# Quantum-style attention over 32 batches: the weighted sum over source heads as a contraction on TensorE, its operands turned through DRAM

## The reference, cut to what matters

```python
qkv = x @ W_qkv.T + b_qkv            # q, k, v: 8 heads of 16 columns each
q, k = entangle(encode(q)), entangle(encode(k))     # complex
for c in range(4):                   # circuits
    scores = g[c] * |conj(q_i) . k_j|^2             # 8 x 8 heads, for each row
    amps = sqrt(softmax(scores, over j) + 1e-12)
    weighted[i, d] = sum_j amps[i, j] * v[j, d]     # <- what the change touches
    final += sup_w[c] * clip(|weighted|, 1e-6, 1) * sign(weighted) * (sign of the sum of v over heads)
y = final @ W_out.T + b_out          # x1 = x + y
```

## Time and profile before

| | |
|---|---|
| median of 3 executions | 2482.29 us (2481.22 to 2492.06) |
| span of the profiled execution | 2447.5 us |
| PE busy | 1901.8 us, 78% |
| DVE busy | 1872.7 us, 77% |
| POOL busy | 1562.1 us, 64% |
| ACT busy | 1264.7 us, 52% |
| chain that ended last, by engine | POOL 30%, issue 25%, DVE 21%, PE 17%, ACT 6% |

### The profile page before, as it was taken

How to read it: one execution, slowest core, us unless ns; L and a number is a source line. 1 busy time by engine, 2 the same in 40 slices (tenths; PEclk the granted TensorE clock), 3 DMA queues, 4 the chain that set the end, 5 groups by cost and what they waited for, 6 DMA issues and landing times.

```text
span 2447.5 us, 42464 instructions
## 1 busy us (share of the span) xinstructions
PE 1901.8 (78%) x14044; PEld 1470.5 (60%) x14044; DVE 1872.7 (77%) x3303; ACT 1264.7 (52%) x2982; POOL 1562.1 (64%) x1233
## 2 busy tenths in 40 slices
PE   1478888888888888888888888888888877968490
PEld 0366666666666666666666666666666654746370
DVE  8989999998999999999999989999998742311010
ACT  2246666555556655555565555555555544423130
POOL 4656666666666666666666666666666215788787
PEclk9889999898999998999998989999989876989795
DMA  3000000000000000000000000000000001233233
GB/s 96 5 5 10 9 9 9 9 9 9 9 9 9 9 9 9 9 9 9 9 9 9 9 9 9 9 9 9 9 9 6 8 10 39 46 41 41 47 36 33
DMA packets 66108, 39.50 MB, mean 16 GB/s; under 512 B 10886, under 2 KB 61967, under 8 KB 66064
## 3 DMA queue, kind: packets, MB, share of 16 engines
q0 software_dynamic: 22528, 16.79, 5.2%
q1 hardware_dynamic: 43490, 22.12, 3.2%
q10 hardware_dynamic: 46, 0.00, 0.0%
HBM read 22.11 MB, written 16.78 MB: 16 GB/s over the span
## 4 chain that ended last, share of the span: by engine, by line
POOL 30%; issue 25%; DVE 21%; PE 17%; ACT 6%; DVEq 1%; POOLq 0%; ACTq 0%; DMA 0%
POOL out_x L1246 7%; POOL arena L481 5%; POOL arena L677 4%; POOL arena L649 4%; DVE arena L831 4%; PE pb L1056 3%; POOL arena L478 2%; POOL arena L1236 2%; PE pa L752 2%; PE pa L779 2%; POOL arena L682 1%; DVE arena L578 1%; DVE arena L583 1%; POOL arena L483 1%; PE pa L1335 1%
## 5 line engine op out<-in xcount | busy, mean ns | idle before, releaser
L771 PE MATMUL pa<-ident,arena 128*128 128x128 f32 x4096 | 531.9, 287 | 56.9 <-DVE arena L649 52.9
L771 PEld LDWEIGHTS pa<-ident,arena 128*128 128x128 f32 x4096 | 504.1, 201 | 74.2 <-DVE arena L649 36.1
L1056 PE MATMUL pb<-ident,arena 128*128 128x128 f32 x1536 | 289.9, 302 | 128.1 <-ACT arena L951 119.0
L1056 PEld LDWEIGHTS pb<-ident,arena 128*128 128x128 f32 x1536 | 187.0, 152 | 246.0 <-issue 158.8
L951 ACT ACTIVATE arena<-pb 128x384 f32<-128x384 f32 x512 | 253.0, 494 | 157.6 <-PE pb L1056 153.8
L677 POOL TENSOR_TENSOR arena<-state,c_cross 128x448 f32<-128x448 f32 x128 | 202.5, 1602 | 203.8 <-DVE state L538 199.1
L669 POOL TENSOR_TENSOR arena<-arena,neg_half 128x32 f32<-128x32 f32 x64 | 264.9, 4158 | 83.8 <-DVE arena L515 83.8
L649 POOL TENSOR_TENSOR arena<-arena 128x1024 f32<-128x1024 f32 x64 | 149.9, 2343 | 197.0 <-PE pa L771 197.0
L944 ACT ACTIVATE arena<-pd,arena 128x256 f32<-128x256 f32 x512 | 245.6, 480 | 0.0
L649 DVE TENSOR_TENSOR arena<-arena 128x1024 f32<-128x1024 f32 x192 | 236.1, 1256 | 2.5 <-PE pa L771 2.2
L1246 POOL DMA_INDIRECT out_x<-arena x128 | 201.9, 1577 | 39.0 <-issue 37.1
(11 more groups left out here) (244 smaller groups left out, 4314.0 us busy)
## 6 DMA issues: line engine op xcount, KB each, us to landing
x_land<-in_L_attn_query SPq DMA_DIRECT2D x32, 128.0 KB, 2.1
arena<-in_L_attn_query SPq DMA_DIRECT2D x32, 128.0 KB, 2.1
out_x<-x SPq DMA_DIRECT2D x32, 128.0 KB, 1.8
xn_scratch<-xn_d SPq DMA_DIRECT2D x32, 128.0 KB, 1.8
w<-in_L_ffn_W SPq DMA_DIRECT2D x1, 2048.0 KB
arena<-xn_scratch,arena POOLq DMA_INDIRECT x128, 2.5
out_x<-arena POOLq DMA_INDIRECT x128, 3.3
arena<-in_L_attn_W_qkv SPq DMA_DIRECT2D x1, 192.0 KB, 2.7
```

What stands on the lines that cost most here:

```text
L771: mm = pe.matmul(pa[:, t, c * P:c * P + P], wprod[:, k % NWP, j * 128:j * 128 + 128], ident[:, :], start=(j == 0), stop=(j == NH - 1))
L1056: mm = pe.transpose(pb[:, j * P:j * P + P], p_raw[:, s % 3, j * P:j * P + P], ident[:, :])
```

## The change

**The sum.** The eight products and their sums by the identity go. The sum over j becomes the contraction itself: `v_diag`, 128 partitions x 16 groups x 256, holds in a group 16 rows of x in block-diagonal form (partition = row and source head j, column = row and d), and `amps_t` holds in the same 128 partitions the 32 amplitudes (circuit, head i) of each. For each of 16 groups, four matmuls with `amps_t` as stationary operand (128 x 32) and 64 columns of `v_diag` as moving operand write four strips of 32 partitions of `pa` (L763 of the changed kernel). The result has (q, circuit, head) on the partitions and (row, d) in the free direction, so W_out is prepared in four parts to match (`wout_q`), and `clipped` is read with a stride of 8 words as stationary operand (L771).

**The turn through DRAM.** SyncE stores v to `v_rows_d` (L1128), reads it back by 16 DMAs of 8 partitions x 16 runs of 64 B into the diagonal blocks (L1134), and reads the amplitudes back by one DMA of 128 x 16 runs of 128 B (L1138). Their store of 128 x 2 KB (L730) is issued by ScalarE, one piece behind the square root. The sign of v is put on at the start of stage C.

**Beside it.** `v_diag` is zeroed once (128 x 4096) at the start. A GpSimd norm waits for the last use of its rstd (`applied`). The four order strings are new: TensorE's work of C and D stands behind the sixteenth head, and the second norm of B comes last on ScalarE.

```diff
-POOL_ORDER = "A1C2B1A4C1B1A2C1D1C1D1"
+POOL_ORDER = "A1C1B1C1A6D1C1B1D1"
...
         def vector_c(v, b):
...
+            v.wait_ge(S("a_venc"), b + 1)
+            yield from L(v.tensor_reduce(v_sum[:, :, :], v_enc[:, :, :].rearrange("p t (i d) -> p t d i", d=HD), AX, ALU.add))
...
+                            ALU.bitwise_xor).then_inc(S("a_signed"), 1)
...
-            v.wait_ge(S("a_amps"), b + 1)
-            for t in range(T):
-                for c in range(NC):
-                    k = t * NC + c
...
-                        weighted(v, t, c).then_inc(S("a_wprod"), 1)
...
         def scalar_c(act, b):
...
             act.wait_ge(S("a_probs"), b + 1)
+            if not (isinstance(b, int) and b == 0):
+                act.wait_ge(S("amps_out"), 16 * b)
...
+            act.wait_ge(S("a_amps"), b + 1)
+            act.dma_start(amps_d, amps[:, :, :, :].rearrange("p t j c -> p (t j c)")).then_inc(S("amps_out"), 16)
+            yield
+            for h in range(2):
+                act.wait_ge(S("a_wsum"), 2 * b + h + 1)
+                act.activation(mag[:, h, :], pa[:, h, :], ACT.Abs).then_inc(S("a_mag"), 1)
...
         def tensor_c(pe, b):
-                    for j in range(NH):
-                        mm = pe.matmul(pa[:, t, c * P:c * P + P], wprod[:, k % NWP, j * 128:j * 128 + 128], ident[:, :],
-                                       start=(j == 0), stop=(j == NH - 1))
...
+            pe.wait_ge(S("v_spread"), 16 * XG * b + 16 * XG)
+            pe.wait_ge(S("amps_spread"), 16 * b + 16)
+            for h in range(2):
+                for g in range(NGRP // 2):
+                    n = NGRP // 2 * h + g
+                    of_row = v_diag[:, n, :].rearrange("p (x d) -> p x d", d=HD)
+                    for q in range(NQ):
+                        mm = pe.matmul(pa[32 * q:32 * q + 32, h, g * 64:g * 64 + 64].rearrange("p (x d) -> p x d", d=DQ),
+                                       amps_t[:, n, :], of_row[:, :, DQ * q:DQ * q + DQ], start=True, stop=True)
+                mm.then_inc(S("a_wsum"), 1)
+                yield
+            pe.wait_ge(S("a_clip"), 2 * b + 2)
+            of_tile = clipped[:, :, :].rearrange("p h (n k) -> p (h n) k", k=T * DQ)
+            for t in range(T):
+                for d in range(DQ):
+                    mm = pe.matmul(pa[:, t, 0:128], of_tile[:, :, t * DQ + d], w_out_t[:, d, :], start=(d == 0), stop=(d == DQ - 1))
...
+        def send_values(sp, b):
...
+            sp.wait_ge(S("a_signed"), b + 1)
+            sp.dma_start(v_rows_d, v_enc[:, :, :].rearrange("p t n -> p (t n)")).then_inc(S("v_out"), 16)
+
+        def spread_values(sp, b):
+            sp.wait_ge(S("v_out"), 16 * b + 16)
...
+            for x in range(XG):
+                sp.dma_start(v_diag[NH * x:NH * x + NH, :, HD * x:HD * x + HD], of_row[x]).then_inc(S("v_spread"), 16)
+
+        def spread_amps(sp, b):
+            sp.wait_ge(S("amps_out"), 16 * b + 16)
+            sp.dma_start(amps_t[:, :, :], amps_d.rearrange("(g x) (t j c) -> (x t j) g c", x=XG // T, t=T, c=CI)).then_inc(S("amps_spread"), 16)
...
             with sp.Fori(3, B - 1) as b:
                 load_x(sp, b + 1)
+                send_values(sp, b - 1)
+                spread_values(sp, b - 1)
+                spread_amps(sp, b - 1)
                 sync_d(sp, b - 3)
                 load_x0(sp, b)
```

More of the change, by code:

```diff
@@ L20 @@
 GW = (NH - 1) * HD
+NQ, DQ = 4, 4
+XG = 16
+NGRP = T * P // XG
+CI = NC * NH
 HID = 384
@@ L179, in build @@
         z_inv = first("z_inv", [P, NC * T * NH])
-        amps = first("amps", [P, NC, T, NH, NH])
-        mag = first("mag", [P, T, NC * P])
-        clipped = first("clipped", [P, T, NC * P])
-        prod = first("prod", [P, T, 3, 1024])
-        wprod = first("wprod", [P, NWP, 1024])
+        amps = first("amps", [P, T, NH, CI])
+        mag = first("mag", [P, 2, 512])
+        clipped = first("clipped", [P, 2, 512])
+        prod = first("prod", [P, 2, 1024])
+        prod_third = first("prod_third", [P, T, 1024])
+        v_diag = first("v_diag", [P, NGRP, XG * HD])
+        amps_t = first("amps_t", [P, NGRP, CI])
         x1 = first("x1", [P, T, E])
@@ L261, in build @@
         wout_s = start("wout_s", [P, 128])
+        wout_q = start("wout_q", [P, NQ, 128])
         pa = psum("pa", [P, T, 512])
@@ L356, in setup_vector @@
             v.memset(xnt_a[:, :], 1.0).then_inc(S("ones_ready"), 1)
+            v.memset(v_diag[:, :, :], 0.0).then_inc(S("v_diag_zero"), 1)
             v.wait_ge(S("ones_ready"), 4)
@@ L468, in setup_tensor @@
                 pe.transpose(pd[:, 3, cs], scaled_down[:, cs], ident[:, :])
-            pe.wait_ge(S("w_out_scaled"), 1)
-            pe.transpose(pb[:, 256:384], wout_s, ident[:, :])
+            pe.wait_ge(S("w_out_scaled"), DQ)
+            for d in range(DQ):
+                pe.transpose(pb[:, d * 128:d * 128 + 128], wout_q[:, d, :], ident[:, :])
             pe.transpose(pc[:, 0:NX], raw_route, ident[0:NX, 0:NX]).then_inc(S("w_turned"), 1)
@@ L474, in build, with norm_scale @@
         heads = lambda a, n=NH: a.rearrange("p (i d) -> p i d", d=HD)
-        def norm_scale(g, u, mv, var, rstd, shift, steps, done):
+        def norm_scale(g, u, mv, var, rstd, shift, steps, done, applied):
+            if not (isinstance(u, int) and u == 0):
+                g.wait_ge(S(applied), 2 * u)
             g.tensor_tensor(var[:, :], mv[:, :, 1], eps_t[:, :], ALU.add).then_inc(S(steps), 1)
@@ L586, in vector_c @@
             yield
-            v4 = v_enc[:, :, :].rearrange("p t (i d) -> p t i d", d=HD)
-            v.wait_ge(S("a_venc"), b + 1)
-            yield from L(v.tensor_reduce(v_sum[:, :, :], v_enc[:, :, :].rearrange("p t (i d) -> p t d i", d=HD), AX, ALU.add))
             v.wait_ge(S("a_pat_sq"), b + 1)
@@ L607, in vector_c @@
             yield
-            v.wait_ge(S("a_amps"), b + 1)
-            for t in range(T):
-                for c in range(NC):
-                    k = t * NC + c
-                    if k and k not in ON_POOL:
-                        yield
-                    if k not in ON_POOL:
-                        if k >= NWP:
-                            v.wait_ge(S("a_wsum"), 8 * b + k - NWP + 1)
-                        weighted(v, t, c).then_inc(S("a_wprod"), 1)
-                    if k == 6:
-                        yield
-                        yield from vector_clip(v, b, 0)
-            yield
-            yield from vector_clip(v, b, 1)
-            yield
+            for h in range(2):
+                yield from vector_clip(v, b, h)
+                yield
             v.wait_ge(S("a_y"), b + 1)
@@ L774, in tensor_c @@
-            for t in range(T):
-                yield
-                pe.wait_ge(S("a_clip"), 2 * b + t + 1)
-                o = pa[:, t, 0:128]
-                for c in range(NC):
-                    mm = pe.matmul(o, clipped[:, t, c * P:c * P + P], w_out_t[:, c, :], start=(c == 0), stop=(c == NC - 1))
+            if not (isinstance(b, int) and b == B - 1):
+                pe.wait_ge(S("a_qkvb"), b + 2)
+            if not (isinstance(b, int) and b == 0):
+                pe.wait_ge(S("x2_ready"), b)
@@ L786, in vector_norm @@
             k0 = count_b[0]
+            if n == 0 and not (isinstance(b, int) and b == 0):
+                v.wait_ge(S("b_scale"), 6 * b - 1)
             for t in range(T):
```

124 lines of the change are left out of this document (58 added, 66 removed).

## The result

The changed kernel takes 2503.88 us (median of 13 runs, 2491.34 to 2514.25), the kernel before 2482.29 (13 runs beside them, 2477.34 to 2492.06). The ratio is 1.0072, with a 95% interval of 1.0054 to 1.009: slower by 0.7%, where I had forecast 2245 us. Over 28 turns x1 comes every 61.50 us (202.65 to 1924.62), before every 60.48.

A forecast was written before the change was run, and what follows sets the result against it. DVE was taken as the bound, though not alone. A laid-out turn cut the period from 60.5 to 52.7 us: 31 periods, 7.8 shorter each, 242 less 5, so 2482 - 237 = 2245 us; range 2195 to 2290, chance 0.52.

The forecast's parts named there:

- From x1 to the eighth minima: Turn's first stretch, stage E: DVE full, 1.8 us of gatings moved behind it, end at t = 30.3 instead of 32.3.
- rival 3: Saved DVE time becomes waits for ACT and GpSimd, and TensorE gets the lower clock more often: 2363 us, chance 0.13.
- The order keeps the same work on DVE: Up to the eighth minima, DVE's work stays, except the FFN's two gatings, 1.8 us, which move behind them.
- its move costs nothing there: Turn's end: B's second norm, now last, is applied at t = 50.1, ahead of TensorE's end, at no cost.
- Sixteen groups with 64 columns at 0.33 are 5.3 us: C's 64 new matmuls on TensorE: 5.3 us a turn, bounds 4.5 and 7.8, ending at t = 45.7.
- I take 2.9: W_out's 16 records near the turn's end: 2.9 us, between 1.95 at full clock and 3.35 in the row shown.
- Rival 2: TensorE reads strided operands slowly: W_out 2 us longer gives 2307 us, a doubled `v_diag` stream in C 2379; chance 0.12.
- It costs nothing: The turn through DRAM is free if amplitudes are in `amps_t` by t = 40.4; cover 1.4 to 3.9 us.
- Rival 1: The amplitudes' 128-B runs cost double, 54 ns each, landing 1.8 us late each turn: 2301 us, chance 0.14.
- rival 4: TensorE stands at its first C matmul waiting for `amps_spread`; at 120 ns a packet 2565 us, slower than before; chance 0.07.
- VectorE's floor: DVE's busy time a period: 55.2 us less 7.5 of its six products, 47.7.
- I let this difference stand: The median lies 35 us above the profiled span of 2447.5; the forecast kept that difference.

The follow-up runs named there:

- e1: The changed kernel plus 24 unused TensorE matmuls a turn, behind C and ahead of the turns of heads 1, 13, 14 and 15: 2304.16 us.
- e6: The changed kernel with only the order altered: B's first norm applied and turned later, behind head 1's copies on ScalarE: 2400.17 us.
- e5: The changed kernel plus 24 unused TensorE matmuls a turn and `clipped` laid out contiguously for W_out's stationary operand: 2274.70 us.
- e3: The changed kernel without the stores, loads and waits of the turn through DRAM, C multiplying zeros: 2499.25 us.
- e4: The kernel before with each product summed over 2 of its 8 heads, 16 product matmuls a turn instead of 64: 2536.57 us.
- e7: The kernel before plus 12 unused matmuls a turn, 4 ahead of C's first product and 8 behind its last: 2462.57 us.
- e12: The changed kernel with contiguous `clipped`, 24 unused matmuls a turn and two more each behind heads 10 and 11: 2290.87 us.

## Why the prediction was wrong

Milestones of a turn in us behind x1, as predicted, in after, and in e1, where the clock is nearly that of before:

| | predicted | after | e1 |
|---|---|---|---|
| eighth minima end | 30.3 | 36.0 | 31.4 |
| o_raw starts | 36.7 | 44.4 | 39.1 |
| C starts on TensorE | 40.4 | 49.4 | 42.9 |
| C's length | 5.3 | 3.1 | 2.1 |
| xn_d ends | 46.6 | 55.1 | 48.6 |
| W_out starts | 48.6 | 57.2 | 50.3 |
| W_out's length | 2.9 | 4.2 | 4.2 |
| next x1 | 52.7 | 61.4 | 54.6 |

**The step that failed** stands in "From x1 to the eighth minima": "DVE is full there, so that counts wholly: t = 30.3". It took stage E's TensorE work at the length that it had at full clock. In after VectorE is not full there: it waits for scores that come at half speed (162.3 us over the kernel, before 53.6, e1 29.6), and 5.7 of the 8.7 missing us are lost by the eighth minima. Another 2.0 are lost up to o_raw and 1.3 up to C. With the clock held up in e1, 4.6 of the 5.7 come back, 0.7 of the 2.0 and 1.2 of the 1.3; for the rest a wrong layout and e1's own half-speed stretch (990 to 997) are not told apart. I had priced 16 us less of TensorE as free or better, and named the lower clock only in rival 3, inside a sentence on other waits, with 119 us of gain left. Its mechanism came true, at a size far outside its price: its 2363 us is still a gain.

**The order.** "The order keeps the same work on DVE" was so; I looked at what moved on VectorE and at the two ends of the turn, and not at B's norm ahead of head 1's copy on ScalarE. Without it the gap is 1.61 us (e6) instead of 2.36; ahead of head 1's turn of before it is 0.68. The other part comes, as I read the traces, from VectorE, which has the second pair's minima 1.5 us later in the new order (7.96 against 6.49 us behind x1), so that ScalarE's exponents and copies wait; no run tests that. Only "its move costs nothing there" was said of B's second norm, at the turn's end.

**C's length.** "Sixteen groups with 64 columns at 0.33 are 5.3 us; bounds are 4.5 and 7.8": 2.13 at full clock and 3.09 in after, below my lower bound. The nearest rows, with 128 and 256 columns, were no floor for 64. The error of 2.2 us hardly counts in the time: behind C TensorE idles for 2.67 us in after until xn_d is there, and in my own layout GpSimd's norm ended together with C at 45.7.

**W_out.** "I take 2.9": 4.15 in after, mostly by the clock, since a contiguous operand would take 3.76 at 1.2 GHz. Rival 2 priced the stationary half at 2 us a turn; it is 0.4 at the lower clock, where after runs, and 2.15 at the full clock (4.20 in e1 less 2.05 in e5), an estimate as far as e1's clock falls on the way, though its loads keep their 0.34 us there. Its other half, the moving operand, shows nowhere. That W_out takes over 3.9 us I had named as a sign of being wrong, and so I had exponents of E that run late; both came.

**The turn through DRAM.** "It costs nothing": right (e3). The load back lands in 3.4 us, inside "3.0 to 4.8", and has 6.8 us of cover where I had 1.4 to 3.9, because C came late. "I take 0.4" for ScalarE's issue: 0.33. Rival 1 (small runs at double cost) and rival 4 (TensorE stands for `amps_spread`) don't occur: L763 waits for the transfer once, 22.8 us in the first C, where nothing covers it (the first x1 still comes at 96.83, before at 96.22), and rival 4's 2565 was right in sign and wrong in cause. The rule of the Trainium skill that I weighed there, DMA: Bandwidth & Descriptors, Specifications, on transfers under 512 B, decided nothing at 256 KB a batch.

**VectorE's floor** of 47.7 was right (47.4), and GpSimd's round of A is not what D's norm waits for: GpSimd idles 3.7 us ahead of it in after. Its 34 came out as 30.1.

**The median above the span.** "I let this difference stand" held. Behind the last x1 before's profiled execution needs 480.7 us, and after's 519.8; the six profiled experiments that I compared (e1, e4, e5, e6, e7, e12), two of them with the old order, lie between 513 and 519, so the profiled run of before seems to have been a quick one there. With these 33 us taken off, the two profiles differ by -13 at the start, +28.6 in the loop and some +6 behind it, together 21.6, and so do the medians. The long waits there in after's profile, which before's lacks (one of 27.07 us at L824, two of 45 at L1306), are put to no engine of the core, and what they wait for stays open.

With the clock kept up and the operand contiguous (e5) the period is 53.76 us and the time 2275, against 52.7 and 2245: the layout of the turn was about right, for a clock that the kernel doesn't get by itself.

## What to carry to other kernels

TensorE's work is not only a cost: before taking some of it away, or reordering work that feeds it, look at the clock row and at the gaps that open ahead of the engine in stages where it is chained with others, and price those stages at both levels. The mean clock alone doesn't tell the price. When a large saving shows in an engine's busy time and not in the span, compare one instruction's duration at two places of the same trace, here 0.60 and 1.06 us for L1041. A few matmuls into unread columns in the right gap are a cheap test of this cause, and can be the remedy; too many lose again.
